# Small inverses applied to the thin factor, one Gram product per chunk, one subtraction per pair: a chunked ridge-attention block with a binarized feed-forward layer

## The chip, the cores and the metric

One core of a Trainium2 chip runs the whole kernel as one program. The metric is device time of one execution in microseconds (us), lower is better. The engines are TensorE (PE: matmuls and transposes, with weight loads listed as PEld), VectorE (DVE), ScalarE (ACT), GpSimd (POOL) and SyncE (SP), which here issues every DMA. Each engine works through its own list in order and waits on semaphores.

## The reference

Four sequences of 1024 rows of 256 numbers go through a layer norm, an attention block and a feed-forward block. Chunks are 128 rows; there are 16 heads of 64.

```python
def step(S, qkv):                      # per head, one chunk after another
    Qc, Kc, Vc = qkv                   # [128, 64] each
    G = Kc.T @ Kc + RIDGE_EPS * I      # 1e-4
    W = jnp.linalg.solve(G, Kc.T @ Vc)
    U = I[:, :8]
    for _ in range(2):
        U, _ = jnp.linalg.qr(W @ U)    # rank 8
    Wr = U @ (U.T @ W)
    S_new = 0.9 * S + Wr
    return (S_new, 0.125 * (Qc @ S_new))
...
x = x + attention(layernorm(x))        # q, k, v = xn @ Wq, Wk, Wv; output @ Wo; its own residual
bw1 = mean(|w1|, per row) * sign(w1)   # w2 alike
x = x + (gelu(layernorm(x) @ bw1.T + b1) @ bw2.T + b2)
```

## The kernel before

The 32 chunks (8 per sequence, which the kernel calls a batch) are worked on singly, in pairs q = 0 to 15, in groups of four g = 0 to 7, and in batches b = 0 to 3. Each engine follows a list that is written out by hand: `PE_ORDER`, `ACT_ORDER`, `DVE_ORDER`, `POOL_ORDER`, `SP_ORDER`. An entry such as `G:14` is one unit of work, and a function of the same table runs it. PE writes a unit into a PSUM place, and ACT or DVE copies it out. The places are three ring banks shared by `XT K V G C X3 H WQ S1 S2`, one double bank `wide` (`ST GI W WT LM`), one `small` (`VS X1 Y YT Z ZT R RP`), one `sum` (`AU`) and one `tok` (`AT`, `O`). A unit waits until the place's unit before it has been copied out.

The way of a chunk:

- `XT` turns the normed rows; `K` and `V` (line 1110, two halves each) make keys and values; `G` (1128) makes the Gram matrices of the 16 heads, `C` the products of keys and values. ACT copies `G` out in two instructions: the leading 32x32 blocks to `lead` (line 690) and the blocks beside them to `rest` (695). SP stores `lead`.
- A pass inverts and factors 128 blocks of 32x32, one on each partition, on DVE: entries `B`, `P:n.0` to `P:n.31` (pivots, lines 916 to 933), `E`, `F`. Passes run in the order (0,0), (0,1), (1,0), (0,2), (1,1), (0,3), (1,2), (1,3), where the first number is 0 for leading blocks and 1 for complements, and the second is the batch. So pass 0 needs `G:0` to `G:7` stored and loaded (`la:0` of SP), pass 1 needs `G:8` to `G:15` (`la:1`), and pass 7 needs `ST:15`.
- For a pair: `VS` and `ST` (1158) make the complement. DVE subtracts it from `rest` (entry `ST`, line 980) in four instructions of 32 partitions each, since for an even chunk and for an odd one the rows lie in other quarters of the partitions. Then `X1`, `GI`, `W`, `WT` (1150) give the solution W, `Y` and `YT` the thin basis, and `Z` = basis-transposed times W the thin right factor (16 heads x 8 rows = 128 rows of 64). DVE masks `Y` and `Z` (984), ACT spreads `YT` and `ZT` (763).
- `LM` (1242, 1246) multiplies the basis into the query weights (the left factor) and into itself: small Gram matrices of the basis, 32 columns wide. `R` (1258) multiplies the right factor into the output weights. Both are stored in DRAM (`sl`, `sr`).
- The small Gram matrices of a batch are loaded (`lm`, four DMAs), inverted on DVE (`M:b.0` to `M:b.7`), stored (`sm`) and loaded as `mb` (`lb`).
- `lp` loads for a pair the right factor, the left factor, the turned rows and the residual. `RP` (1269), one per chunk, multiplies the small inverse into the right factor, 256 columns wide; `AU` (1278) adds the chunk to the running operator; `AT` (1287) applies it.
- `X3`, `H` (1305) and `O` (1317) are the feed-forward part, per group, in half precision with a high and a low part.

In the trace each single-precision matmul is two records, so `R`, 16 matmuls, is 32 records, and `RP`, four matmuls, is 8.

Of the kernel before, what the change touches and what calls it, by code (L numbers as in the profile page):

```python
# [1348 lines left out]
```

## Time and profile before

| | |
|---|---|
| time, three runs | 868.2 us median (865.0 to 872.72) |
| profiled execution | 869.31 us, of which span of the core 867.5 us |
| mean granted TensorE clock | 0.974 |
| PE busy | 771.0 us, 89% |
| DVE busy | 581.7 us, 67% |
| ACT busy | 445.0 us, 51% |
| chain that ended last | PE 31%, DVE 28%, issue 15%, SPq 11%, DMA 10%, ACT 5% |

Busy time counts the union of an engine's instructions; the granted clock is the share of full speed that TensorE got. The chain is followed back from the last instruction, at each step to what released it; "SPq" is time in which SP issued DMAs. Places and times below are counted from the span's start.

### The profile page before, as it was taken

The numbers are of one execution on the slowest core, as the hardware profiler recorded it, in microseconds if no ns is written. First come the engines' busy times: TensorE is split into PE (matmuls) and PEld (weight loads), VectorE is DVE, ScalarE is ACT, GpSimd is POOL, SyncE is SP. The second block draws the span as 40 slices with busy tenths as digits, with TensorE's granted clock in tenths as the row PEclk, the third lists the DMA queues.
The fourth block names the chain that finished last, engine by engine and source line by source line (L and its number), as shares of the span: only waits on it lengthen the run. The fifth ranks groups of instructions, "written<-read, shape, count | busy, mean of one in ns | idle before, by whom it ended". The sixth has DMA issues, their size and how long they took to land.

```text
span 867.5 us, 29412 instructions
## 1 busy us (share of the span) xinstructions
PE 771.0 (89%) x12784; PEld 499.1 (58%) x12784; DVE 581.7 (67%) x1578; ACT 445.0 (51%) x888; POOL 79.6 (9%) x60
## 2 busy tenths in 40 slices
PE   1899999799999989998789889689989999999886
PEld 1355555455455467565566656476667686756563
DVE  3210994289999999999799976679935332565463
ACT  3654554355335345444344436645646647566463
POOL 3100003000300302003003002000020000000000
PEclk9999999899999989999998999999999999999999
DMA  9735313746147645564755656735175632242200
GB/s 265 230 86 76 110 52 114 129 120 137 25 106 125 134 77 109 140 107 125 126 121 120 176 150 197 138 76 121 42 218 108 169 87 81 85 140 74 87 20 30
DMA packets 267315, 100.50 MB, mean 116 GB/s; under 512 B 225457, under 2 KB 260529, under 8 KB 266161
## 3 DMA queue, kind: packets, MB, share of 16 engines
q1 hardware_dynamic: 267184, 98.62, 47.1%
q8 instruction: 100, 1.64, 0.9%
q14 instruction: 31, 0.25, 0.1%
HBM read 53.35 MB, written 45.22 MB: 114 GB/s over the span
## 4 chain that ended last, share of the span: by engine, by line
PE 31%; DVE 28%; issue 15%; SPq 11%; DMA 10%; ACT 5%; POOL 2%; POOLq 0%; DVEq 0%; ACTq 0%
DVE outer L924 11%; DVE ax L933 9%; PE wide L1150 6%; PE tok L1317 5%; PE ring L1305 3%; PE ring L1110 3%; DVE comp L980 2%; PE sum L1278 2%; DVE rd L916 2%; PE tok L1287 2%; SPq L454 2%; PE small L1258 2%; DMA inv_d<-xo 2%; SPq L436 1%; PE ring L1128 1%
## 5 line engine op out<-in xcount | busy, mean ns | idle before, releaser
L1110 PE MATMUL ring<-wkv,xt 128*128 128x512 f32 x512 | 248.5, 625 | 7.4 <-ACT keys L677 3.5
L924 DVE SCALAR_TENSOR_TENSOR outer<-ax,rd 128x448 f32<-128x448 f32 (+15 forms) x368 | 186.1, 533 | 8.8
L933 DVE TENSOR_TENSOR ax<-ax,outer 128x448 f32<-128x448 f32 (+15 forms) x368 | 163.4, 471 | 4.4
L1110 PEld LDWEIGHTS ring<-wkv,xt 128*128 128x128 f32 x512 | 93.7, 195 | 103.8 <-issue 88.4
L1035 DVE TENSOR_TENSOR wkv<-ht,wkv 128x512 f16<-128x512 f32 x64 | 43.6, 689 | 41.7 <-ACT wkv L830 41.3
L579 POOL TENSOR_TENSOR root<-rdc,pos_half 128x32 f32<-128x32 f32 x8 | 43.8, 5474 | 291.4 <-DVE rdc L941 291.4
L683 ACT COPY vals<-ring 128x512 f32<-128x512 f32 x64 | 37.4, 586 | 63.9 <-PE ring L1110 63.5
L1317 PE MATMUL tok<-s2t,wkv 128*128 128x256 f16 x512 | 63.0, 283 | 5.3 <-DVE wkv L1035 3.9
L1305 PE MATMUL ring<-y,s1t 128*128 128x512 f16 x256 | 63.4, 384 | 0.7 <-ACT ht L823 0.6
L823 ACT ACTIVATE ht<-ring,b1c,alpha 128x512 f32<-128x512 f32 x64 | 49.1, 777 | 27.2 <-PE ring L1305 19.6
L1317 PEld LDWEIGHTS tok<-s2t,wkv 128*128 128x128 f16 x512 | 50.8, 101 | 17.3 <-DVE wkv L1035 5.2
L916 DVE RECIPROCAL rd<-ax 128x1 f32<-128x1 f32 x256 | 40.9, 160 | 4.2
L980 DVE TENSOR_TENSOR comp<-rest,wide 32x256 f32<-32x256 f32 x64 | 26.7, 417 | 22.1 <-PE wide L1158 14.0
L865 DVE BATCH_NORM_STATS2 stats<-xg 128x6 f32<-128x256 f32 x32 | 11.2, 414 | 43.1 <-DMA xg<-in_L_attn_x_dram 43.1
L1305 PEld LDWEIGHTS ring<-y,s1t 128*128 128x128 f16 x256 | 23.7, 99 | 28.4 <-issue 3.8
L830 ACT CAST wkv<-ht 128x512 f16<-128x512 f32 x64 | 39.0, 618 | 1.0
L1150 PEld LDWEIGHTS wide<-xf 64*64 64x64 f32 x1024 | 32.1, 138 | 10.5 <-issue 8.2
L1287 PE MATMUL tok<-ac_xn 128*128 128x256 f32 x128 | 34.4, 391 | 4.1 <-ACT ac_xn L799 3.4
L1242 PE MATMUL wide<-wqt,yp 128*32 128x256 f32 x512 | 33.9, 383 | 4.1 <-ACT cut L715 3.6
L1278 PE MATMUL sum<-rp,la 128*128 128x256 f32 x128 | 35.5, 400 | 1.8 <-issue 1.3
L1150 PE MATMUL wide<-xf 64*64 64x64 f32 x1024 | 34.3, 223 | 2.8 <-DMA xf<-inv_d 2.0
L1150 PE MATMUL wide<-giw,resl_c 64*64 64x64 f32 x1024 | 35.0, 225 | 0.5 <-DMA resl_c<-c_d 0.5
(139 smaller groups left out, 1108.4 us busy)
## 6 DMA issues: line engine op xcount, KB each, us to landing
c_d<-cross SPq DMA_DIRECT2D x32, 256.0 KB, 3.2
inv_d<-xo SPq DMA_DIRECT2D x8, 1024.0 KB, 4.7
resl_c<-c_d SPq DMA_DIRECT2D x16, 512.0 KB, 4.9
lm_d<-lm SPq DMA_DIRECT2D x16, 288.0 KB, 3.6
xg<-in_L_attn_x_dram SPq DMA_DIRECT2D x8, 512.0 KB, 4.6
res_d<-xg SPq DMA_DIRECT2D x8, 512.0 KB, 2.7
xt_d<-xt SPq DMA_DIRECT2D x8, 512.0 KB, 3.3
xx<-inv_d SPq DMA_DIRECT2D x64, 64.0 KB, 2.2
```

What stands on the lines that cost most here:

```text
L579: V.tensor_tensor(root[:], rdc[:], pos_half[:], ALU.pow).then_inc(root_ready, 1)
L823: S.activation(ht[:, t % 2], src[:], ACT.Gelu, bias=b1c[:, t:t + 1], scale=alpha1[:, t:t + 1]).then_inc(done, 1)
L916: at = note(V.reciprocal(r, a[:, k, k:k + 1]))
L924: at = note(V.scalar_tensor_tensor(out=t, in0=a[:, k, r0:r1].unsqueeze(2).broadcast_to([P, rows, cols]), scalar=r, in1=a[:, k, r0:HALF + k ...
L933: ends.append(note(V.tensor_tensor(rest, rest, t, ALU.subtract)))
L980: V.tensor_tensor(comp[rows], rest[rows, (2 * q + u) % KEPT], sides[rows], ALU.subtract).then_inc(comp_ready, 1)
L1110: ins = mm(dst[:], xt[:, g % 2, t, P * k:P * (k + 1)], weight[:, t, BANK * j:BANK * (j + 1)], start=t == 0, stop=t == KT - 1)
L1150: ins = mm(dst[half(s), at:at + size], left(s, u, h), right_of(s, u, h), start=True, stop=True)
L1278: ins = mm(dst[:, DM * t:DM * (t + 1)], la[:, n, u, P * t:P * (t + 1)], rp[:, c % 2], start=c % CPB == 0 and t == 0, stop=c % CPB == CPB - ...
L1287: ins = mm(dst[:, 0:DM], xn[:, n, t, P * u:P * (u + 1)], ac[:, c % 2, t], start=t == 0, stop=t == KT - 1)
L1305: ins = mm(dst[:], s1t[:, k, P * t:P * (t + 1)], y3[:, part, k], start=k + part == 0, stop=k + part == KT)
L1317: ins = mm(dst[:, DM * k:DM * (k + 1)], hid[:, part, t, at:at + P], s2t[:, t], start=k + t + part == 0, stop=t + part == FT, skip_group_ch ...
```

## The change

Five things change, and all five orders are written anew.

1. `RP` is gone. `Z` is copied by ACT to `zk` (both halves of the double buffer hold a batch), `ZP` multiplies the small inverse into it (8 matmuls of 32x32 by 64 columns for a pair), DVE masks that, and `ZT` turns it. `R` now makes the finished right factor; ACT scales it into `rp`, and `AU` reads it there. The stores and loads of the right factor through DRAM are gone.
2. `LM`'s small Gram matrices come from one 128x128 by 128 matmul per chunk on a packed copy `ypc` of the turned basis, which ACT makes with a third copy in `YT`. They are stored apart (`m_d`), with a pad row that puts the diagonal blocks at a constant pitch, so one DMA loads them where four did.
3. `G` is copied out to `rest` in four instructions of 32 partitions, so that the rows which the two chunks' complements need lie in one slot.
4. DVE then makes the complement of a pair in one 128-partition subtraction.
5. The orders: both x groups are loaded first, the query weights are turned later, and so on.

```diff
             def gram_out(c):
...
-                    act.wait_ge(comp_ready, 4 * (q + 1))
-                S.copy(rest[:, c % KEPT], blocks[:, :, HALF * (1 - u):HALF * (2 - u)]).then_inc(done, 1)
+                    act.wait_ge(comp_ready, q + 1)
+                across = blocks[:, :, HALF * (1 - u):HALF * (2 - u)]
+                at = 2 * (c // 2) % KEPT
+                for s in range(2):
+                    S.copy(rest[block_rows(s, u), at], across[block_rows(s, u)])
+                    ins = S.copy(rest[block_rows(s, 1 - u), at + 1], across[block_rows(s, 1 - u)])
+                ins.then_inc(done, 1)
...
             def comp_out(q):
-                    for s in range(2):
-                        rows = block_rows(s, 1 - u)
-                        V.tensor_tensor(comp[rows], rest[rows, (2 * q + u) % KEPT], sides[rows], ALU.subtract).then_inc(comp_ready, 1)
+                V.tensor_tensor(comp[:], rest[:, 2 * q % KEPT + 1], sides, ALU.subtract).then_inc(comp_ready, 1)
...
             def left_out(q):       # PE
-                        for f in range(4):
-                            rows, h, at = slice(32 * f, 32 * (f + 1)), 2 * f + odd, BANK * u + DM
-                            ins = mm(dst[rows, at:at + 32], yp[:, u, h], yp[:, u, h], start=False, stop=odd == 1,
-                                     skip_group_check=True, tile_position=(0, 32 * f))
+                for u in range(2):
+                    at = BANK * u + DM
+                    ins = mm(dst[:, at:at + P], ypc[:, u], ypc[:, u], start=True, stop=True, skip_group_check=True)
...
-            def applied(c):
-                dst, done = begin("RP", c)
-                n, u = c // 2 % 2, c % 2
-                pe.wait_ge(apply_loaded[n], 64 * uses_of_slot(c // 2))
-                pe.wait_ge(minv_loaded, 16 * (c // CPB + 1))
-                for f in range(4):
-                    rows = slice(32 * f, 32 * (f + 1))
-                    ins = mm(dst[rows, 0:DM], mb[rows, c % CPB], ra[rows, n, u], start=True, stop=True,
-                             tile_position=(32 * f, 32 * f))
+            def applied(q):
+                dst, done = begin("ZP", q)
+                copied(pe, "Z", q)
+                pe.wait_ge(minv_loaded, 16 * (2 * q // CPB + 1))
+                for u in range(2):
+                    for f in range(4):
+                        rows = slice(32 * f, 32 * (f + 1))
+                        ins = mm(dst[rows, HD * u:HD * (u + 1)], mb[rows, (2 * q + u) % CPB],
+                                 zk[rows, q // PAIRS_B % 2, q % PAIRS_B, u], start=True, stop=True, tile_position=(32 * f, 32 * f))
...
             def right_out(q):      # ACT
                 src, done = begin("R", q)
-                act.wait_ge(r_stored, 16 * q)
-                S.copy(rr[:].rearrange("p u n -> p (u n)"), src[:]).then_inc(done, 1)
+                if q >= 2:
+                    computed(act, "AU", 2 * q - 3)
+                else:
+                    computed(act, "G", NCH - 1)
+                    computed(act, "C", NCH - 1)
+                for u in range(2):
+                    ins = S.activation(rp[:, q % 2, u], src[:, DM * u:DM * (u + 1)], ACT.Copy,
+                                       scale=DECAY ** -((2 * q + u) % CPB))
+                ins.then_inc(done, 1)
...
             def load_apply(q):
-                sp.wait_ge(r_stored, 16 * (q + 1))
-                sp.wait_ge(lm_stored, 16 * (q + 1))
+                sp.wait_ge(left_stored, 16 * (q + 1))
...
-                load(ra[:, n], r_d[both].rearrange("c p n -> p c n")).then_inc(apply_loaded[n], 16)
...
 PE_ORDER = """
-XT:0.0 XT:0.1 WQ:0 WQ:1 K:0.0 K:0.1 K:1.0 K:1.1 K:2.0 K:2.1 G:0 XT:1.0 K:3.0 G:1 XT:1.1 K:3.1 K:4.0 G:2 K:4.1
+XT:0.0 XT:0.1 XT:1.0 XT:1.1 K:0.0 K:0.1 K:1.0 K:1.1 K:2.0 G:0 K:2.1 G:1 K:3.0 K:3.1 K:4.0 K:4.1 K:5.0 K:5.1
```

PE at the very start, before the change (`ident,giw` is a turn of the query weights, `wkv,xt` a key unit, `keys` a Gram unit; x2 of 128x512 is one K unit):

```order
L1103 MATMUL ring<-ident,xh 128x128 x8
L1071 MATMUL ring<-ident,giw 128x128 x8
L1110 MATMUL ring<-wkv,xt 128x512 x12
L1128 MATMUL ring<-keys 64x64 x16
L1103 MATMUL ring<-ident,xh 128x128 x4
```

and with the change:

```order
L1113 MATMUL ring<-ident,xh 128x128 x16
L1120 MATMUL ring<-wkv,xt 128x512 x10
L1138 MATMUL ring<-keys 64x64 x16
L1120 MATMUL ring<-wkv,xt 128x512 x2
L1138 MATMUL ring<-keys 64x64 x16
```

All four turns of rows now come first, and no turn of the query weights stands ahead of the keys.

SP around the load for pass 1 (`ax<-lead_d`), before the change; `resl_c<-c_d` is the load for the first pair's `W`, which waits for the turns of the second feed-forward weight, and `c_d<-cross` here is the store of `C:8`:

```order
L428 DMA inv_d<-xo 128x2048
L401 DMA lead_d<-lead 32x8x32 x2
L436 DMA xx<-inv_d 32x8x64 x8
L401 DMA lead_d<-lead 32x8x32 x4
L478 DMA resl_c<-c_d 128x16x64
L405 DMA c_d<-cross 128x8x64
L418 DMA ax<-lead_d 128x32x32
L436 DMA xx<-inv_d 32x8x64 x4
```

and with the change:

```order
L431 DMA inv_d<-xo 128x2048
L404 DMA lead_d<-lead 32x8x32 x4
L439 DMA xx<-inv_d 32x8x64 x4
L421 DMA ax<-lead_d 128x32x32
L439 DMA xx<-inv_d 32x8x64 x4
L408 DMA c_d<-cross 128x8x64
L481 DMA resl_c<-c_d 128x16x64
```

The load for pass 1 has moved ahead of four side loads, of `C:8`'s store and of the load for `W`.

ACT around the first Gram units, with the change (before, each `lead` row was followed by one row `rest<-ring 128x256`):

```order
L688 COPY lead<-ring 128x256
L696 COPY rest<-ring 32x256
L697 COPY rest<-ring 32x256
L696 COPY rest<-ring 32x256
L697 COPY rest<-ring 32x256
L675 COPY x<-ring 128x512
```

The ring bank of a Gram unit is given back after the fifth instruction instead of the second.

## Rows read from the trace of the kernel before

**Rows 1.** Busy time by stretches; columns: stretch, length, engines' busy us, PEclk, DMA share, GB/s.

```profile
core 0: us, PE busy (x) PEld busy (x) DVE busy (x) ACT busy (x) POOL busy (x), PEclk, DMA share, GB/s
0.00:50.00 50.00, 27.36 (x159) 14.99 (x160) 12.13 (x58) 28.80 (x64) 11.92 (x22) 1.00 0.75 236
50.00:169.00 119.00, 112.32 (x1150) 61.73 (x1148) 56.99 (x167) 57.62 (x113) 11.35 (x6) 1.00 0.42 90
169.00:530.00 361.00, 325.02 (x6558) 208.36 (x6562) 328.35 (x892) 163.86 (x335) 38.97 (x20) 0.96 0.54 120
530.00:650.00 120.00, 104.84 (x2190) 75.67 (x2171) 84.94 (x228) 68.09 (x137) 10.05 (x6) 0.96 0.56 130
650.00:867.50 217.50, 201.46 (x2746) 138.33 (x2743) 99.30 (x235) 126.60 (x242) 7.30 (x7) 0.98 0.32 88
sum 867.50, PE 771.00 PEld 499.07 DVE 581.70 ACT 444.96 POOL 79.58; mean PE 154.20 PEld 99.81 DVE 116.34 ACT 88.99 POOL 15.92
```

**Rows 2.** Timeline, DVE: starts of passes 0 and 1, and `ST:15`.

```profile
86.11 0.20 DVE L911 TENSOR_SCALAR ax<-ax 128x32 f32<-128x32 f32 x1 [23.63 <-DMA ax<-lead_d]
...
169.13 0.20 DVE L911 TENSOR_SCALAR ax<-ax 128x32 f32<-128x32 f32 x1 [8.46 <-DMA ax<-lead_d]
...
530.56 1.76 DVE L980 TENSOR_TENSOR comp<-rest,wide 32x256 f32<-32x256 f32 x4
```

**Rows 3.** Timeline, PE: the waits of the start, in brackets.

```profile
14.79 1.94 PE L1103 MATMUL ring<-ident,xh 128*128 128x128 f32 x8 [14.79 <-DVE xh L903]
19.75 1.97 PE L1071 MATMUL ring<-ident,giw 128*128 128x128 f32 x8 [3.02 <-DMA giw<-in_L_attn_Wq_dram]
21.51 9.02 PE L1110 MATMUL ring<-wkv,xt 128*128 128x512 f32 x16
34.02 3.70 PE L1110 MATMUL ring<-wkv,xt 128*128 128x512 f32 x8 [3.49 <-ACT keys L677]
```

**Rows 4.** Timeline, PE: `G:15`, and the second side unit with what follows.

```profile
149.63 1.15 PE L1128 MATMUL ring<-ra 128*64 128x64 f32 x32
...
170.15 1.08 PE L1158 MATMUL small<-rest,xx 32*32 32x32 f32 x64 [4.67 <-DMA xx<-inv_d]
171.16 3.78 PE L1110 MATMUL ring<-wkv,xt 128*128 128x512 f32 x4
```

**Rows 5.** Timeline, SP: DMA issues between `G:15` and the load for pass 1.

```profile
155.09 1.94 SPq L401 DMA_DIRECT2D lead_d<-lead  x4
157.28 1.06 SPq L478 DMA_DIRECT2D resl_c<-c_d  x1
158.39 1.43 SPq L405 DMA_DIRECT2D c_d<-cross  x1
159.91 1.11 SPq L418 DMA_DIRECT2D ax<-lead_d  x1
```

**Rows 6.** Timeline, PE: back-to-back units; a unit's price is start to next start.

```profile
591.25 1.93 PE L1258 MATMUL small<-wo,zp 128*32 128x256 f32 x32
593.00 0.61 PE L1242 MATMUL wide<-wqt,yp 128*32 128x256 f32 x8
...
594.97 0.63 PE L1203 MATMUL small<-wt,w 128*32 128x64 f32 x32
...
600.11 0.44 PE L1209 MATMUL small<-ident,zm 128*128 128x128 f32 x2
600.38 1.89 PE L1305 MATMUL ring<-y,s1t 128*128 128x512 f16 x8
...
609.43 0.63 PE L1269 MATMUL small<-ra,mb 32*32 32x256 f32 x8
610.00 1.04 PE L1305 MATMUL ring<-y,s1t 128*128 128x512 f16 x4
```

**Rows 7.** Groups by line: busy us, mean ns of one, idle before it.

```profile
L980 DVE TENSOR_TENSOR comp<-rest,wide 32x256 f32<-32x256 f32 x64 | 26.7, 417 | 22.1 <-PE wide L1158 14.0 <-DMA comp_d<-comp 3.0 <-issue 3.0
L727 ACT COPY xf<-small 32x256 f32<-32x256 f32 x64 | 23.2, 363 | 7.7 <-PE small L1158 6.4
L695 ACT COPY rest<-ring 128x256 f32<-128x256 f32 x32 | 12.1, 379 | 0.0
```

More of the change, by code:

```diff
@@ L14 @@
 CPB = SEQ // P
+PAIRS_B = CPB // 2
 NCH = BATCH * CPB
@@ L526, in load_apply @@
                 both = slice(2 * q, 2 * q + 2)
[L527 to L528 removed]
+                load(la[:, n], left_d[both].rearrange("c p n -> p c n")).then_inc(apply_loaded[n], 16)
                 load(xn[:, n], xt_d[g][:, :, 2 * P * n:2 * P * (n + 1)]).then_inc(apply_loaded[n], 16)
@@ L770, in basis, with left_out @@
                     computed(act, "LM", q - 1)
-                spread(yp, src).then_inc(done, 1)
+                spread(yp, src)
+                S.copy(ypc[:].rearrange("p u n -> p (u n)"), src[:, 0:2 * P]).then_inc(done, 1)
             def right(q):
+                src, done = begin("Z", q)
+                if q >= 2 * PAIRS_B:
+                    computed(act, "ZP", q - 2 * PAIRS_B)
+                S.copy(zk[:, q // PAIRS_B % 2, q % PAIRS_B].rearrange("p u n -> p (u n)"), src[:, 0:2 * HD]).then_inc(done, 1)
+            def left_out(q):
+                src, done = begin("LM", q)
+                act.wait_ge(left_stored, 16 * q)
+                act.wait_ge(m_stored, 16 * q)
+                S.copy(lm[:], src[:].rearrange("p (u n) -> p u n", u=2)[:, :, 0:DM + P]).then_inc(done, 1)
+            def applied(q):
                 src, done = begin("ZT", q)
@@ L777, in right @@
                 spread(zp, src).then_inc(done, 1)
-            def left_out(q):
-                src, done = begin("LM", q)
-                act.wait_ge(lm_stored, 16 * q)
-                S.copy(lm[:], src[:].rearrange("p (u n) -> p u n", u=2)[:, :, 0:DM + 32]).then_inc(done, 1)
             def right_out(q):
                 src, done = begin("R", q)
-                act.wait_ge(r_stored, 16 * q)
-                S.copy(rr[:].rearrange("p u n -> p (u n)"), src[:]).then_inc(done, 1)
-            def applied(c):
-                src, done = begin("RP", c)
-                if c >= 2:
-                    computed(act, "AU", c - 2)
-                S.activation(rp[:, c % 2], src[:, 0:DM], ACT.Copy, scale=DECAY ** -(c % CPB)).then_inc(done, 1)
+                if q >= 2:
[7 more added lines that the diff above has]
+                ins.then_inc(done, 1)
             def operator(c):
@@ L991, in basis, with applied @@
                 masked(ym[:], src, done)
-            def right(q):
-                src, done = begin("Z", q)
+            def applied(q):
+                src, done = begin("ZP", q)
                 if q:
@@ L1226, in right @@
                 thin(dst, done, yp, w)
-            def right_turned(q):
-                dst, done = begin("ZT", q)
-                copied(pe, "Z", q)
-                turned_factors(dst, done, zm)
             def left_out(q):
```

283 lines of the change are left out of this document (143 added, 140 removed).

## Prediction

> **What bounds the kernel now.** I read the busy time by stretches first [rows 1]. PE is idle for 867.5 - 771.0 = 96.5 us: 22.6 in the first 50 us, 6.7 up to 169, 36.0 from 169 to 530, 15.2 up to 650 and 16.0 after it. DVE works through 328.35 of the 361 us from 169 to 530, 91%, and through less than half of the last 217. So two engines take turns. Up to 530 the pivot passes on DVE set the pace and PE waits for them; after `ST:15` at 530.56 [rows 2], which lets the last pass begin, PE has a backlog and works at 93%.
>
> Then the timeline of DVE: pass 0 starts at 86.11 after 23.63 us of waiting, pass 1 at 169.13, at the end of a second wait, both for loads of leading blocks [rows 2]. These two dates are not set by DVE. For the first, the timeline of PE [rows 3]: it begins at 14.79, waits 3.02 us for the query weights, starts the keys at 21.51, and waits 3.49 us for ACT, which is held by magnitudes of feed-forward weights that it needs much later. For the second: `G:15` starts on PE at 149.63 and is done at 150.8 [rows 4], but the load that it allows is issued at 159.91 [rows 5]. Between them SP issues the last lead stores up to 157.0, then the load for `W` and the store of `C:8`, which waits for its product. So up to nine of the 18 us from `G:15` to pass 1 are the order on SP.
>
> The sum is made against the profiled execution: 869.31 us, 1.8 over its span and 1.1 over the median of 868.2.
>
> **The change, part by part.** Prices are starts of back-to-back units [rows 6].
>
> *PE work.* One `RP` unit is 610.00 - 609.43 = 0.57 us; 32 go, 18.2 us. `ZP` has no row: 16 matmuls' worth of records, 64 columns, against `Y` with 32 records and 64 columns, 0.63 us at most. Between 0.15 and 0.63 us, I take half, 0.3; 16 units, 4.8 us. `LM`: its group in the page looks costly, but the unit takes 594.97 - 593.00 = 1.97 us and `R`, the same without the small Gram matrices, 593.00 - 591.25 = 1.75: they cost 0.22 us, being packed beside the others. The two full matmuls in their place are four records; a turn of two records of the same size costs 600.38 - 600.11 = 0.27, so 0.54 a unit and +0.32 net, 16 times, 5.1 us more. That part of the change is a loss on PE; between 0 and 10 us, I take 5. PE work falls by 18.2 - 4.8 - 5.1 = 8.3 us.
>
> The Trainium skill, "TensorEngine Tiling (Array Packing)", section Instruction Overhead, says that every matmul carries about 60 cycles of overhead, so that few columns cost no less than 60. By that, an estimate from the page, 16 records of `ZP` would take 0.4 us and the cut of PE work would be 1.6 us smaller; the row of `Y` (32 records in 0.63) is below it.
>
> *DVE work.* The four subtractions of a pair take 1.76 us [rows 2], one of 32x256 417 ns [rows 7]. The length is set by the 256 elements, not by the partitions: on ACT 32x256 takes 363 ns and 128x256 379 [rows 7]. So one is left, 0.42, and 1.34 us go, 16 times 21.4 us, 15 of them inside the DVE-bound stretch. Masks: 16 go, 16 come.
>
> *ACT work.* Four copies of 363 ns for one of 379 [rows 7]: +1.07 us for each `G`, 34 us in all. `ypc`, `zk` and the wider `lm` add about 0.4, 0.4 and 0.2 us a pair, `R` in two pieces replaces two `RP` copies and `rr` is gone: +7 together. ACT rises from 445 to about 486 us. What hides it: in 50 to 169, where `G:4` to `G:15` lie, ACT is busy for 57.6 of 119 us [rows 1]; K, K, G is 1.9 + 1.9 + 1.1 us on PE [rows 3, 4] against about 3.0 on ACT with the new copies. Without that cover it costs 34 us, the second rival.
>
> The Trainium skill, "ScalarE: Activation LUTs", section Rules for kernel authors, budgets about 0.3 us for an activation and 0.83 ns an element. By it, an estimate, a copy of 256 elements would be 0.51 us and the extra 49 us instead of 34; the rows show 0.36 for this copy, and the sum keeps them.
>
> *SP.* 12 issues for small loads, 16 stores and 16 loads of the right factor go, 16 stores come: 28 fewer, at 0.36 to 0.5 us each [rows 5]. I book nothing: after 650 PE has its backlog as cover. The moved load for pass 1 does count, next.
>
> *The start.* x group 1 is loaded before weights, all four turns come first, the query weights leave the head of PE, and the magnitudes come later on ACT. The first product can come about 4 us earlier (DVE's statistics of x group 1 no longer wait behind the weights), the 3.02 us are gone, so the keys start near 16 instead of 21.5; the 3.49 are gone too, and one turn of query weights less (0.9) stands before `C:1`. The four-piece copy of `G:7` gives 1.1 back. Pass 0 starts near 86.1 - 9 = 77 (bounds 74 and 84).
>
> *Pass 1.* From `C:1` to `G:15` PE has the same work in both orders (16 K, 8 G and 6 C each; 13 V against 12). So `G:15` comes near 141, its copies and stores end at 144, four side loads stand ahead of `la:1`, and 169.1 - 159.9 = 9.2 us pass from issue to start: pass 1 starts near 151 to 153, 17 us earlier. Pass 0 (51 us) is over by then, so nothing else is late. Also gone is the wait of 4.67 us at 170.15, after which the next key unit took 3.78 us instead of 1.9 [rows 4]: TensorE was granted its lower clock, 1.2 GHz.
>
> *To ST:15, the meeting point.* On DVE it is 532.3 - 169.1 = 363 us from pass 1 today. Off go 15 x 1.34 = 20, and about 5 for what now stands behind `ST:15` (five short pivots, two additions). 363 - 25 = 338, from 152: 490. On PE it is 532.3 - 21.5 = 511 from the first key; off go 4 us of work (most `RP` lie later), 3.5 and 4.7 of waits and 2 of lower clock, 497 from 16: 513, if its other 30 us of waits stay. They are mostly waits for DVE, which is now 20 us earlier; I let half of them go: 498. I take 498.
>
> *From ST:15 to the end* 335 us remain today. PE still has 13 `R` units where it had 11 and 25 `RP`; `ZP`, `ZT` and `LM` included, 4 us less. The new chain `ZP`, mask, `ZT`, spread, `R`, `AU` is about 4 us longer than `RP`, `AU`, once a batch, but starts from data that is on the chip; FFN units cover it. 331.
>
> Sum: 498 + 331 = 829 us of span, 830.8 of time; against the median 830.
>
> **Rivals.**
>
> *Only PE's own gains count* (chance 0.2). If the 30 us of waits stay, because they come from ACT, DMA and PSUM places and not from DVE, `ST:15` comes at 513: 844 + 1.8 = 846. For it: eight in ten busy tenths on PE even in the DVE stretch. Against it: DVE is busy for 91% there.
>
> *The Gram copies turn ACT and the ring into the bound; slower* (0.07). A Gram unit now holds one of three banks 1.1 us longer. If PE stands still for that time at each of 32 units, 34 us come on PE's path, and the DVE passes start later, not earlier; the start gains 5.5, the rest of DVE's relief is not used: 869 + 34 - 5.5 - 8.3 = 889. It decides from about 1.1 us of stall in 13 of 32 units on, where the 14 us of PE's certain gains are used up. Against it ACT's idle half [rows 1].
>
> *A wash, within 1%* (0.08). The longer ACT and `ZP` chains cost PE waits at pair after pair, 2 us each, 32 us, and eat the 38. Time 862.
>
> *All waits for DVE go* (0.12): `ST:15` at 490 and 10 us of the 31 us of idle after 530 too: 490 + 321 + 2 = 813.
>
> *The forecast* (0.53), own range 820 to 842.
>
> **How the numbers follow.** Range 808 to 856: it holds the forecast, the rival of PE's own gains and the fast case to their edges, and leaves out the two slow ones and a little on the fast side. About 1% is what a measurement of this kernel can tell from no change. Faster by over 1%: 0.53 + 0.2 + 0.12 = 0.85; within 1%: 0.08; slower: 0.07.
>
> **What the next profile would show.** Right: pass 0 starts before 80 and pass 1 before 156; DVE's subtraction is 16 of about 420 ns; `ST:15` lies before 505; PE idle from 150 to 500 is under 30 us; the idle of PE ahead of key units for ACT `rest` stays under 8 us in all. Wrong: key units wait for ACT `rest` again and again (second rival); or DVE waits for PE at `ST` or `Y` entries for tens of us while PE still waits elsewhere (first). What would break the forecast most is the assumption on the 335 us after `ST:15`: if the new orders leave PE without work there at the pairs of batch 3, the gain is given back at the end.

## The result, and the profile after

The changed kernel takes 824.7 us (median of four runs, 823.0 to 831.3), the kernel before 869.6 beside it (865.0 to 872.7): a ratio of 0.950, 95% interval 0.943 to 0.957. The profiled execution has a span of 821.2 us against 867.5. Forecast were 830 us. Medians here are those of the executions in the chip's fast state: one execution each of both_late, old_four_copies and the kernel before lay in a slower one and is left out.

Busy time by the same stretches as in [rows 1]; the columns are stretch, length, busy us of PE, PEld, DVE, ACT and POOL with their instructions, granted clock, DMA share, GB/s:

```profile
0.00:50.00 50.00, 38.08 (x210) 19.96 (x211) 12.12 (x58) 30.18 (x72) 11.93 (x22) 1.00 0.73 227
50.00:169.00 119.00, 106.70 (x1138) 60.89 (x1137) 63.85 (x185) 75.47 (x155) 11.35 (x6) 0.96 0.44 97
169.00:530.00 361.00, 337.57 (x6640) 217.19 (x6638) 321.83 (x890) 202.36 (x423) 42.41 (x21) 0.97 0.58 127
530.00:650.00 120.00, 115.31 (x2497) 88.26 (x2490) 82.81 (x223) 77.87 (x164) 8.88 (x7) 1.00 0.48 115
650.00:821.20 171.20, 158.53 (x1864) 108.42 (x1862) 78.33 (x177) 97.31 (x188) 4.78 (x4) 0.99 0.22 64
sum 821.20, PE 756.20 PEld 494.73 DVE 558.93 ACT 483.20 POOL 79.35; mean PE 151.24 PEld 98.95 DVE 111.79 ACT 96.64 POOL 15.87
```

PE is idle for 65.0 us where it was idle for 96.5: 11.9, 12.3, 23.4, 4.7 and 12.7 us by stretch. Its work is 14.8 us less, ACT's 38 us more, DVE's 23 us less. The same view of after, split at the meeting point that the prediction used, `ST:15`:

```profile
0.00:499.59 499.59, 455.26 (x7693) 281.48 (x7693) 373.04 (x1055) 288.98 (x615) 58.89 (x47) 0.98 0.56 129
499.59:821.20 321.61, 300.93 (x4644) 213.25 (x4644) 185.90 (x476) 194.22 (x386) 20.46 (x13) 0.98 0.36 91
```

and of before:

```profile
0.00:530.56 530.56, 465.26 (x7871) 285.24 (x7872) 398.00 (x1117) 250.34 (x512) 62.79 (x48) 0.97 0.53 124
530.56:867.50 336.94, 305.74 (x4914) 213.83 (x4914) 183.70 (x461) 194.63 (x377) 16.79 (x13) 0.97 0.40 103
```

Up to `ST:15` 31.0 us are gained, 10.0 of work and 21.0 of idle time on PE; behind it 15.3, of which 4.8 are work and 10.5 idle time.

The timeline of DVE, answering to [rows 2]: starts of passes 0 and 1, the complements `ST:0` and `ST:1`, and `ST:15`.

```profile
86.27 0.20 DVE L923 TENSOR_SCALAR ax<-ax 128x32 f32<-128x32 f32 x1 [13.26 <-DMA ax<-lead_d]
...
160.00 0.20 DVE L923 TENSOR_SCALAR ax<-ax 128x32 f32<-128x32 f32 x1 [14.49 <-DMA ax<-lead_d]
...
162.68 0.42 DVE L990 TENSOR_TENSOR comp<-rest,wide 128x256 f32<-128x256 f32 x1 [0.20 <-DVE ax L945]
...
173.08 0.42 DVE L990 TENSOR_TENSOR comp<-rest,wide 128x256 f32<-128x256 f32 x1 [1.68 <-issue]
...
499.59 0.42 DVE L990 TENSOR_TENSOR comp<-rest,wide 128x256 f32<-128x256 f32 x1
```

`ST:15` is 31 us earlier, pass 1 9 us, pass 0 not at all. The gain grows to 25.3 us at the end of pass 4, falls to 17.0 at the end of pass 5 and is 31.0 at `ST:15` (dates of `ST:3` and of the passes' ends, lines 941 and 953, from the same timelines):

| | ST:3 | end of pass 0 | 1 | 2 | 3 | 4 | 5 | ST:15 |
|---|---|---|---|---|---|---|---|---|
| before | 200.1 | 137.2 | 229.0 | 284.5 | 338.8 | 393.2 | 460.7 | 530.6 |
| after | 190.5 | 137.3 | 214.6 | 266.5 | 317.1 | 367.9 | 443.7 | 499.6 |
| four_subs, below | | 138.3 | 221.2 | 276.6 | 328.9 | 381.2 | 456.8 | 518.1 |

From the end of pass 4 to the end of pass 5 DVE waits for 14.6 us with the change and for 4.2 before it; the longest of these waits are for the load of pass 5 (4.9 us), for a `ZP` unit (3.9) and at `ST:11` (3.8). The last step of the row is in part a matter of order: before, `ST:15` stands behind the whole of pass 6, with the change ahead of its last five pivots. The end of pass 6 itself comes 20.7 us earlier (505.6 against 526.3), the start of pass 7 37.7 (510.2 against 547.9).

The start on PE, answering to [rows 3], and the one long wait behind it:

```profile
13.67 1.97 PE L1113 MATMUL ring<-ident,xh 128*128 128x128 f32 x8 [1.54 <-DVE xh L915]
15.44 1.06 PE L1120 MATMUL ring<-wkv,xt 128*128 128x512 f32 x1
...
147.88 3.50 PE L1120 MATMUL ring<-wkv,xt 128*128 128x512 f32 x4 [8.56 <-ACT rest L697]
```

Groups by line, for [rows 7] (busy us, mean ns of one, idle before it):

```profile
L990 DVE TENSOR_TENSOR comp<-rest,wide 128x256 f32<-128x256 f32 x16 | 6.7, 419 | 7.9 <-issue 5.5 <-PE wide L1168 1.8 <-DVE ax L945 0.4
...
L697 ACT COPY rest<-ring 32x256 f32<-32x256 f32 x64 | 23.3, 363 | 0.8
...
L775 ACT COPY ypc<-small 128x256 f32<-128x256 f32 x16 | 6.4, 398 | 0.0
...
L1261 PE MATMUL small<-zk,mb 32*32 32x64 f32 x256 | 6.9, 220 | 1.8 <-DMA mb<-minv_d 1.8
```

The subtraction is 16 instructions of 419 ns. The copies of `rest`, 64 each on lines 696 and 697, take 363 ns of ACT for 32 partitions.

### The profile page after: what moved, and what is told of

Its sections match the earlier page's. It is cut to its first block, busy times and chain, and to the rows that moved or that the text cites. A ratio compares the mean times of both kernels' runs of the same rounds, so it can differ in the third digit from the quotient of the medians.

```text
span 821.2 us, 28518 instructions
## 1 busy us (share of the span) xinstructions
PE 756.2 (92%) x12336; PEld 494.7 (60%) x12336; DVE 558.9 (68%) x1530; ACT 483.2 (59%) x1000; POOL 79.4 (10%) x60
## 4 chain that ended last, share of the span: by engine, by line
PE 49%; DVE 23%; DMA 8%; issue 8%; ACT 5%; SPq 4%; POOL 1%; DVEq 0%; ACTq 0%; POOLq 0%
PE ring L1120 13%; DVE outer L936 8%; PE wide L1160 7%; DVE ax L945 6%; PE tok L1327 6%; PE ring L1138 3%; PE ring L1315 3%; PE wide L1247 3%; PE tok L1297 2%; PE small L1278 2%; PE sum L1288 2%; DMA ax<-lead_d 2%; DMA ax<-comp_d 2%; PE small L1168 2%; DVE rd L928 1%
## 5 line engine op out<-in xcount | busy, mean ns | idle before, releaser
L1120 PE MATMUL ring<-wkv,xt 128*128 128x512 f32 x512 | 245.0, 620 | 9.0 <-ACT rest L697 8.8
L1045 DVE TENSOR_TENSOR wkv<-ht,wkv 128x512 f16<-128x512 f32 x64 | 42.9, 688 | 37.9 <-ACT wkv L842 37.7
L1315 PEld LDWEIGHTS ring<-y,s1t 128*128 128x128 f16 x256 | 23.4, 98 | 27.6 <-ACT ht L835 2.2
L1160 PE MATMUL wide<-resl_c,giw 64*64 64x64 f32 x1024 | 34.5, 224 | 4.7 <-DMA resl_c<-c_d 4.7
L1160 PEld LDWEIGHTS wide<-resl_c,giw 64*64 64x64 f32 x1024 | 32.4, 139 | 7.4 <-issue 5.2
L1160 PEld LDWEIGHTS wide<-giw,resl_c 64*64 64x64 f32 x1024 | 31.1, 135 | 6.2 <-issue 4.2
```

Of the source, the lines that this page charges most:

```text
L1045: V.tensor_tensor(hid[:, 1, t], ht[:, t % 2], hid[:, 0, t], ALU.subtract).then_inc(h_low, 1)
L1120: ins = mm(dst[:], xt[:, g % 2, t, P * k:P * (k + 1)], weight[:, t, BANK * j:BANK * (j + 1)], start=t == 0, stop=t == KT - 1)
L1160: ins = mm(dst[half(s), at:at + size], left(s, u, h), right_of(s, u, h), start=True, stop=True)
L1315: ins = mm(dst[:], s1t[:, k, P * t:P * (t + 1)], y3[:, part, k], start=k + part == 0, stop=k + part == KT)
```

## The experiments

Twelve kernels were run. Medians are beside a kernel before of 869.0 to 870.5 us.

| kernel | built on | median us | ratio to before, 95% interval |
|---|---|---|---|
| al_late | after | 821.8 | 0.941 to 0.948 |
| turn_late | after | 824.1 | 0.943 to 0.951 |
| both_late | after | 824.9 | 0.942 to 0.953 |
| four_subs | after | 842.3 | 0.966 to 0.972 |
| pe_filler | after | 839.0 | 0.963 to 0.969 |
| both_costs | after | 855.2 | 0.980 to 0.989 |
| trip_back | after | 832.9 | 0.951 to 0.962 |
| packed_gram | after | 823.8 | 0.944 to 0.952 |
| packed_al | after | 821.4 | 0.941 to 0.948 |
| old_four_copies | before | 873.7 | 1.000 to 1.008 |
| old_one_sub | before | 865.7 | 0.990 to 0.997 |
| old_load_early | before | 871.4 | 0.999 to 1.003 |

### Do the dates of passes 0 and 1 matter?

The prediction had pass 0 at 77 and pass 1 at 152; they came at 86.3 and 160.0. What held them is plain in the trace. SP of after, in front of the load for pass 0 (line 421):

```profile
65.80 0.51 SPq L378 DMA_DIRECT2D alpha_d<-alpha  x1
74.00 0.34 SPq L380 DMA_DIRECT2D alpha2r<-alpha_d  x1
74.38 0.93 SPq L404 DMA_DIRECT2D lead_d<-lead  x2
75.35 0.45 SPq L408 DMA_DIRECT2D c_d<-cross  x1
79.61 0.60 SPq L421 DMA_DIRECT2D ax<-lead_d  x1
```

Entry `al` stores the scales of the second feed-forward weight and waits until they have landed, 7.7 us, before it issues their load; the last two stores of leading blocks stand behind it. In before it stood ahead of `gs:3` and was over by 61.7. ACT, before pass 1:

```profile
144.28 1.90 ACT L708 COPY xo<-xo 128x1024 f32<-128x1024 f32 x1 [8.26 <-DVE xo L959]
...
147.85 0.37 ACT L688 COPY lead<-ring 128x256 f32<-128x256 f32 x1
...
149.37 0.36 ACT L697 COPY rest<-ring 32x256 f32<-32x256 f32 x1
```

Line 708 is `T:0`, which waits for pass 0 and stands ahead of `G:14` and `G:15` in ACT's order. Both were done on PE by 137.4, but their banks are held until 147.8 and 149.7, and PE's next key unit waits 8.56 us and then takes 3.50 us instead of 1.9, in the lower granted clock.

Three kernels move these entries:

```diff
 SP, al_late
-x:4 al gs:7 cs:1 la:0 cs:2
+x:4 gs:7 cs:1 la:0 al cs:2
 ACT, turn_late                      (both_late: both edits)
-T:0 G:14 G:15
+G:14 G:15 T:0
 SP, turn_late
-gs:13 sa:0 gs:14 gs:15 lx:0 la:1 lx:1
+gs:13 gs:14 gs:15 la:1 sa:0 lx:0 lx:1
```

> The changed kernel; only SP's entry al (store of alpha2, a wait for it to land, load of alpha2r) is moved from ahead of the last lead stores of batch 0 to behind the load for pass 0. Theory 1, the SP order took the 9 us of the start: in the changed kernel al held SP for 8 us, the last lead store was issued at 74.4 though its data lay ready at 69.1; now pass 0 starts near 80 instead of 86.3, pass 1 near 154 instead of 160 since its ACT turn is also earlier, and the time falls by 3 to 7 us against the changed kernel (ratio to before 0.942 to 0.947). Theory 2, pass 0 has slack since PE is the bound from 50 us on: pass 0 starts earlier but the time stays within 1.5 us.

> The changed kernel; ACT's turn of pass 0's result (T:0) stands behind G:14 and G:15 instead of ahead of them, and SP's la:1 ahead of sa:0. Theory 1, T:0 made ACT wait 8.3 us for pass 0 with two full Gram banks behind it, so PE stood 8.6 us and then ran at the lower clock, and pass 1 began 10 us late: now the wait is gone, pass 1 starts near 150, ST:15 near 490, time 5 to 10 us below the changed kernel. Theory 2, the waits only move (side products need the turn anyway): PE idle moves to the first side unit, pass 1 starts earlier, the time changes by less than 2 us.

> Both moves. If the passes set the pace up to ST:15, pass 0 starts near 80 and pass 1 near 148, and the time is 8 to 14 us below the changed kernel (near 812). If PE is the bound, at most the 8.6 us of its standing wait can be won back, and this kernel is no faster than the one with the late turn alone.

Both entries gave their dates back: in both_late pass 0 starts at 79.35 and pass 1 at 148.84. The time did not follow: 821.8 us in al_late, 824.1 in turn_late and 824.9 in both_late, with 824.7 in after. DVE of both_late shows where 11 us went:

```profile
79.35 0.20 DVE L923 TENSOR_SCALAR ax<-ax 128x32 f32<-128x32 f32 x1 [5.63 <-DMA ax<-lead_d]
...
148.84 0.20 DVE L923 TENSOR_SCALAR ax<-ax 128x32 f32<-128x32 f32 x1 [6.05 <-DMA ax<-lead_d]
...
161.67 0.42 DVE L990 TENSOR_TENSOR comp<-rest,wide 128x256 f32<-128x256 f32 x1 [10.34 <-issue]
...
172.07 0.42 DVE L990 TENSOR_TENSOR comp<-rest,wide 128x256 f32<-128x256 f32 x1 [1.67 <-issue]
...
201.69 0.20 DVE L923 TENSOR_SCALAR ax<-ax 128x32 f32<-128x32 f32 x1
```

`ST:0` is subtracted at 161.67 (162.68 in after): DVE's order puts it behind the first pivot of pass 1, so a pass that starts 11 us earlier stands still for 10.34 us at it. Its product comes only 1.0 us earlier, because PE itself waits for the side blocks `xx`, which come from pass 0's result:

```profile
156.24 0.75 PE L1168 MATMUL small<-rest,xx 32*32 32x32 f32 x64 [3.26 <-DMA xx<-inv_d]
...
159.76 1.78 PE L1168 MATMUL wide<-xx 32*32 32x64 f32 x64
```

The row of DVE at 201.69, the start of pass 2, is 1.0 us earlier than in after (202.68). So the wait moved from the load to the first complement, and a start of pass 1 earlier than at 160 brings nothing.

The same move in the kernel before:

```diff
-gs:13 lx:0 lx:1 gs:14 gs:15 l3:0 cs:8 la:1 lx:2
+gs:13 lx:0 gs:14 gs:15 la:1 lx:1 l3:0 cs:8 lx:2
```

> The kernel before; only SP's load for pass 1 stands ahead of the last side load, of the load for W and of the store of C:8. Theory: pass 1 starts near 160 instead of 169, and since DVE sets the pace up to ST:15 the time falls by 5 to 9 us. Rival: PE and the products that the subtractions wait for keep their dates, DVE waits later, under 2 us.

Pass 1 started at 165.5 instead of 169.1 and PE waited 6.8 us for `xx` instead of 4.7; time 871.4, no difference. DVE waited for the product of `ST:1`, in before and then in old_load_early:

```profile
176.47 1.76 DVE L980 TENSOR_TENSOR comp<-rest,wide 32x256 f32<-32x256 f32 x4 [2.73 <-issue]
```

old_load_early:

```profile
179.78 1.76 DVE L980 TENSOR_TENSOR comp<-rest,wide 32x256 f32<-32x256 f32 x4 [9.66 <-PE wide L1158]
```

The old order of DVE has two pivots of pass 1 ahead of `ST:1`, so a pass that starts earlier only waits longer there. The new order has five. With it DVE is busy from 160.0 to 171.4 in after, with these five and `ST:0`, and then waits 1.68 us for `ST:1`. Had pass 1 started at 169.1 as in before, the same work would have ended at 180.5, an estimate, and `ST:1` would come 7.4 us later than at 173.1. So the date of pass 1 has no more than 1.7 us of slack towards later, and nothing is won by an earlier one. No run delayed the pass or changed DVE's order alone.

For al_late alone the four times (821.0 to 822.6) all lie below those of after (823.0 to 831.3), and with packed Gram products the same edit gives 821.4 against 823.8; the intervals overlap, and both_late, which holds the same edit, lies at 824.9. So 2 to 3 us are possible but not shown.

### DVE's subtraction

```diff
-                V.tensor_tensor(comp[:], rest[:, 2 * q % KEPT + 1], sides, ALU.subtract).then_inc(comp_ready, 1)
+                for k in range(4):
+                    rows = slice(HALF * k, HALF * (k + 1))
+                    ins = V.tensor_tensor(comp[rows], rest[rows, 2 * q % KEPT + 1], sides[rows], ALU.subtract)
+                ins.then_inc(comp_ready, 1)
```

> The changed kernel with the subtraction of a pair in four instructions of 32 partitions again (four copies of the Gram matrix stay). It puts 16 x 1.34 = 21 us back on DVE, 20 of them before the last pass begins. DVE theory: ST:15 comes 15 to 20 us later than 499.6, time 12 to 18 us longer (837 to 843). PE theory: DVE has room, under 4 us.

842.3 us, 17.6 more than after, for 16 x 1.3 = 21 us of DVE work. `ST:15` comes 18.5 us later, of which 1.0 is there at the start of pass 0 (DVE of four_subs):

```profile
518.10 1.71 DVE L992 TENSOR_TENSOR comp<-rest,wide 32x256 f32<-32x256 f32 x4
```

So in the new orders most of the DVE work that is added between pass 1 and `ST:15` is time of the kernel. In the old orders the same part was tried by itself, with the copies it needs (old_one_sub), and the copies alone (old_four_copies):

```diff
 both
-                S.copy(rest[:, c % KEPT], blocks[:, :, HALF * (1 - u):HALF * (2 - u)]).then_inc(done, 1)
+                four copies of 32 partitions each
 old_one_sub
-                    for s in range(2):
-                        rows = block_rows(s, 1 - u)
-                        V.tensor_tensor(comp[rows], rest[rows, (2 * q + u) % KEPT], sides[rows], ALU.subtract).then_inc(comp_ready, 1)
+                V.tensor_tensor(comp[:], rest[:, 2 * q % KEPT + 1], sides, ALU.subtract).then_inc(comp_ready, 1)
```

> The kernel before; only the copy of a Gram matrix to rest is split into four of 32 partitions: 32 x 1.1 = 35 us more on ACT, each Gram unit's bank held 1.1 us longer. Forecast's theory, hidden under PE: 0 to 5 us longer. Rival of the slower outcome: 14 to 34 us longer.

> The kernel before with its own orders, and parts 3 and 4 of the change: four copies of 32 partitions into a common slot, one subtraction a pair. DVE loses 21 us, ACT gains 35. If DVE sets the pace to ST:15 and ACT has room, the time falls by 8 to 16 us even in the old orders. If the old orders tie DVE to dates set by PE, by under 4 us, and the gain of the changed kernel needs the new orders.

The copies alone cost 0.4% (873.7 us; 0 to 0.8%), far from the 34 us of the second rival. With the subtraction it is 865.7, 0.3 to 1.0% faster than before: 8 to 9 us better than the copies alone, by the medians about half of the 17.6 that the same subtraction is worth in the new orders. Both are loose: by the ratios and their intervals 5 to 14 us here and 9 to 23 there, so the half isn't shown. The timelines of DVE (`ST:15`) and then of PE of old_one_sub:

```profile
521.16 0.41 DVE L983 TENSOR_TENSOR comp<-rest,wide 128x256 f32<-128x256 f32 x1
```

PE, its waits in brackets:

```profile
33.44 5.40 PE L1113 MATMUL ring<-wkv,xt 128*128 128x512 f32 x8 [3.68 <-ACT keys L677]
...
47.41 5.40 PE L1113 MATMUL ring<-wkv,xt 128*128 128x512 f32 x8 [3.51 <-ACT x L677]
```

The old start is tight on ACT: two key units wait for its copies for 3.68 and 3.51 us and then take 5.40 us; in before the same waits are 3.49 us ([rows 3]) and 1.34, and the units take 3.70. Pass 0 starts at 92.07, 6 us late. `ST:15` still comes 9.4 us earlier than in before. But these waits belong to the copies and don't explain what the subtraction lacks: old_four_copies has them too (3.78 and 3.39 us, pass 0 at 91.66). DVE of old_four_copies:

```profile
539.20 1.76 DVE L984 TENSOR_TENSOR comp<-rest,wide 32x256 f32<-32x256 f32 x4
```

That is 18.0 us behind `ST:15` of old_one_sub, as much as in the new orders. The two profiled executions (877.3 and 860.9 us) lie 3.6 us above and 4.7 below the medians of their kernels, so up to 8 us of the 18 can be chance. Whether the old orders let less of DVE's relief through stays open.

### PE's work

```diff
             def applied(q):                      # pe_filler: ahead of each ZP
                 for u in range(2):
+                    for f in range(4):
+                        rows = slice(32 * f, 32 * (f + 1))
+                        mm(dst[rows, 256 * u:256 * (u + 1)], mb[rows, (2 * q + u) % CPB], zk[rows, ...][:, 0:256], ...)
```

> The changed kernel; ahead of each ZP the products of two old RP units (8 matmuls of 32x32 by 256 columns) are computed and overwritten: 16 x 1.13 = 18 us of PE work back, all but three of the units behind ST:15; nothing else waits for them. If PE is the bound behind ST:15, the time rises by 13 to 18 us. If the end of the kernel is set by chains over DVE, ACT and DMA, by under 5 us.

839.0 us, 14.3 more. The products cost less than was expected (PE of pe_filler, one pair):

```profile
577.86 1.07 PE L1261 MATMUL small<-zk,mb 32*32 32x256 f32 x16
578.74 0.40 PE L1267 MATMUL small<-zk,mb 32*32 32x64 f32 x16
```

They take 0.88 us from start to start, 14.1 us in all and not 18, and PE's busy time rises by 14.5 us, from 756.2 to 770.7. So 14.1 us of added PE work cost 14.3 us of time, one for one. In the profile 5.2 us appear before `ST:15` (504.79), 1.3 of them already at the start of pass 0, the rest behind it. Both costs together:

> The changed kernel with two earlier experiments put together: the complement of a pair in four subtractions again (+21 us of DVE work), and eight products of 256 columns ahead of each ZP (+18 us of PE work; their results are overwritten by the product that follows). Singly they cost 18 and 14 us. Theory: up to ST:15 both engines are near the bound in turns, so the costs mostly add: 32 us less some that hide behind each other, 850 to 856 us. What then remains to the kernel before, 13 to 19 us, is what the written orders give alone. Rival: each relief is only real while the other is there (one meeting point, the later engine decides); then the sum is far less than additive, 842 to 846 us, and the orders give 25 us. The starting phase as the main cause would want at least 17 us to remain, since pass 1 starts 9 us and pass 0 not at all earlier than before.

855.2 us, 30.6 above after; the single costs sum to 31.9. They add, as the theory had it, and the rival of one late engine deciding is out by 9 us at least.

14 to 15 us remain between this kernel and before. That is what is left for the new orders, the dropped traffic, and the costs of the change that stay in. PE is busy for 778.4 us in this kernel against 771.0 in before, ACT for 483.1 against 445.0 and DVE for 581.0 against 581.7: it is faster with more work.

### The traffic of the right factor

```diff
+                load(r_d[both].rearrange("c p n -> p c n"), lm[:, :, 0:DM]).then_inc(r_stored, 16)       # sl
...
+                load(ra[:, n], r_d[both].rearrange("c p n -> p c n")).then_inc(apply_loaded[n], 16)     # lp
```

> The changed kernel with the traffic of the right factor through DRAM put back: per pair one more store of 256 KB behind LM's stores and one more load of 256 KB into an unused buffer, on which AU waits together with the others (the data are those of the left factor). 32 more DMA issues on SP, 8.4 MB. The prediction booked nothing for them, since PE has a backlog after ST:15. By that 823 to 828 us. Rival: PE's idle time after ST:15 fell from 31 to 17 us because SP and the DMA engines are less loaded there; then 14 us come back, 834 to 840 us.

832.9 us, by the medians 8.2 more than after. The two intervals overlap (0.951 to 0.962 and 0.943 to 0.957), but al_late, turn_late, both_late and the two packed kernels, which also do without this traffic, all lie at 821 to 825 us, so a cost is likely; its size is loose. The prediction had booked nothing. The loss isn't all where the rival wanted it. Busy time from the end of pass 5 to `ST:15`, of trip_back and then of after:

```profile
447.43:507.15 59.72, 52.40 (x1364) 37.51 (x1359) 52.14 (x135) 28.79 (x62) 7.54 (x4) 0.94 0.70 188
```

after:

```profile
443.70:499.59 55.89, 50.79 (x1365) 36.87 (x1359) 52.05 (x136) 28.58 (x62) 7.54 (x4) 0.97 0.62 166
```

The same work takes 59.7 us instead of 55.9, with the DMA engines busy for 0.70 instead of 0.62 and the granted clock at 0.94 instead of 0.97: it is the stretch in which the first stores of factors, the loads for `AU` and the last complements meet. Another 3.0 us come behind `ST:15` (324.7 against 321.6), where PE waits 2.2 us for `resl_c<-res_d` and 1.1 for `xf<-inv_d`, 0.5 and nothing in after. The other 3.7 us of the profiled difference are there by the end of pass 5, 2.7 of them by the end of pass 1, ahead of all this traffic: dates vary by that much from run to run (pass 0 starts at 87.9 here, 87.7 in both_costs, 85.8 in packed_gram and 86.3 in after). So I read 5 to 8 us for the traffic.

### The Gram product of the basis

PE of after, one `LM` unit with the units around it, for [rows 6]:

```profile
592.07 1.91 PE L1247 MATMUL wide<-wqt,yp 128*32 128x256 f32 x32
593.91 0.71 PE L1251 MATMUL wide<-ypc 128*128 128x128 f32 x4
594.55 0.43 PE L1261 MATMUL small<-zk,mb 32*32 32x64 f32 x16
594.91 1.26 PE L1327 MATMUL tok<-s2t,wkv 128*128 128x256 f16 x10
```

The unit takes 594.55 - 592.07 = 2.48 us against 1.97 before, `ZP` 0.36. The kernel packed_gram makes the Gram matrices by 32 columns again, but writes each at its diagonal place, so that the single load and everything else stay:

```diff
-                S.copy(ypc[:].rearrange("p u n -> p (u n)"), src[:, 0:2 * P]).then_inc(done, 1)
...
-                for u in range(2):
-                    at = BANK * u + DM
-                    ins = mm(dst[:, at:at + P], ypc[:, u], ypc[:, u], start=True, stop=True, skip_group_check=True)
+                        for f in range(4):
+                            rows, h, at = slice(32 * f, 32 * (f + 1)), 2 * f + odd, BANK * u + DM + 32 * f
+                            ins = mm(dst[rows, at:at + 32], yp[:, u, h], yp[:, u, h], start=False, stop=odd == 1, ...)
```

> The changed kernel with the basis's small Gram matrices made as before, 16 products of 32 columns a pair beside the left factor's, but written at the places of the diagonal blocks, so that the single load stays; the copy ypc on ACT goes. PE work falls by 16 times the difference of the LM units, 2.48 against 1.97 us, 8.2 us, ACT by 6.4 us. By the slope that the filler experiment gave (14 us of time for 18 us of PE work) 6 to 8 us faster than the changed kernel: 817 to 820 us. Rival: the LM units lie where PE waits anyhow or where other work fills in, then no change, 823 to 826 us.

> The kernel packed_gram with SP's entry al moved behind the load for pass 0, as in al_late. If al_late's 3 us are real and independent, 3 us faster than packed_gram: 814 to 817 us. If pass 0's date is worth nothing, the same as packed_gram within 1 us.

PE of packed_gram, the start of one `LM` unit (lines 1246 and 1250) and the `ZP` unit behind it:

```profile
591.60 0.61 PE L1246 MATMUL wide<-wqt,yp 128*32 128x256 f32 x8
...
593.69 0.42 PE L1261 MATMUL small<-zk,mb 32*32 32x64 f32 x16
```

The unit is 593.69 - 591.60 = 2.09 us, so 0.39 less, 6.2 in all; PE's busy time falls from 756.2 to 751.5 us and ACT's from 483.2 to 478.8. The time is 823.8, 0.9 below after: too little to tell from nothing, and below the 4.7 us by which PE's busy time fell, though the work that pe_filler added was paid in full. Why this cut brings nothing isn't shown. packed_al (821.4) is the fastest kernel of the study by its median, 0.3 us before al_late: no difference. Neither is shown to beat the changed kernel; packed_gram shows only that the full product brings nothing that 16 small ones do not.

## Why the prediction was right, and where it wasn't

The date of `ST:15` (498 forecast, 499.6 found) and the time (830, 824.7) came out, but not by all of the steps.

| step | forecast | found |
|---|---|---|
| keys start on PE | 16 | 15.4 |
| pass 0 starts | 77 (74 to 84) | 86.3 |
| pass 1 starts | 151 to 153 | 160.0 |
| worth of pass 1's earlier start | 17 us in the bound on DVE | about 7 us, an estimate |
| DVE's subtraction | 16 x 420 ns, 21.4 us off | 16 x 419 ns; DVE 22.8 us less |
| worth of it | most of 20 us | 17.6 us |
| `ST:15` | 498 | 499.6 |
| `ST:15` to the end | 331 | 321.6 |
| PE's work (busy time) | -8.3 | -14.8 |
| `LM` unit / `ZP` unit | +0.32 / 0.3 us | +0.51 / 0.36 us |
| ACT busy | 486 | 483.2 |
| PE's wait for ACT `rest` | under 8 us | 8.8 us, all but 0.2 in one place |
| traffic of the right factor | 0 | 5 to 8 us, likely |

*The start.* Two steps are wrong. "Pass 0 starts near 86.1 - 9 = 77" moved the products and forgot SP: the keys start 6.1 us earlier as forecast, but `al` had been put between them and the load. "G:15 comes near 141, its copies and stores end at 144" was too late for PE (137.4) and too early for ACT, whose next entry waits for pass 0. In both the order of a third engine was on the path, and the prediction had walked only two of them. al_late and turn_late confirm both causes by their dates.

*And why it didn't matter.* The step "338 us from pass 1 to `ST:15`, from 152: 490" took the stretch as a sum of DVE work from pass 1's start. From 160.0 it was 339.6 us, as forecast. But with pass 1 at 148.8 it is 350.3 us (both_late, `ST:15` at 499.1): an earlier pass waits for PE's products at `ST:0` and `ST:1`. So the 8 us by which pass 1 missed its date cost nothing, and 490 could not be had by that date. At the end of pass 1 the gain is 14.4 us. Of it 3.4 are the earlier product of `ST:1`; 6.3 are the three more pivots that DVE's new order has ahead of `ST:1`, for which the start at 160.0 made room; 4.0 are three cheaper subtractions. Behind `ST:1` DVE waits for 0.2 us in before and for nothing in after. That is read from the traces; no run undid this part of the orders.

*PE's way to `ST:15`*, 498 from the key at 16, is what the forecast took, and here two errors cancel. From the first key to `ST:15` PE took 509.1 us before; 482 were booked and 484.2 found. PE's busy time in it fell by 10.0 us where 6 were booked, its waits by 14.9 (47.5 to 32.6) where 23 were; 8.6 of the waits that are left are the one behind `T:0`. And beside the two waits that the prediction named there were 39 us of others and not 30. That the date came out to 1.6 us is in part luck.

*DVE's relief* was right in mechanism and size: 16 x 1.34 forecast, 17.6 us of time by four_subs.

*Two readings of rows* don't hold, without weight for the sum: PE works at 93% behind 650 [rows 1], but at 91% behind `ST:15` (305.74 of 336.94 us); and the issues in [rows 5] take 0.49 to 1.43 us each, not 0.36 to 0.5.

*Prices.* `ZP` at 0.36 us lies above the 0.3 of the sum and below the 0.4 that the prediction worked out by the Trainium skill. The Trainium skill, "TensorEngine Tiling (Array Packing)", section Instruction Overhead, puts about 60 cycles on every matmul however few its columns; the trace comes near it for `ZP` (16 records of 64 columns in 0.36 us, 22 ns each, 54 cycles at 2.4 GHz), but not for `VS`, whose 64 records of 32 columns take 0.68 us from start to next start at 158.86 in after, 11 ns or 26 cycles each. So the sum is right to go by rows. The copies of `rest` cost 363 ns. The Trainium skill, "ScalarE: Activation LUTs", section Rules for kernel authors, would have given 0.51, an estimate; its budget is for activations, these are plain copies, and the trace decides.

*PE's work.* `RP` went as priced (32 x 0.57). By the unit prices found, the sum is -18.2 + 5.8 + 8.2 = -4.2, yet PE's busy time fell by 14.8 us. The other ten lie in units that the change leaves as they are: their 11504 records sum to 760.7 us by groups before and to 750.0 after. Some 4 to 5 come from the granted clock, 0.978 over 821.2 us against 0.974 over 867.5: that is 36 us at the lower of the two clocks instead of 45. Why the rest of these units is shorter is open. What a microsecond of PE work is worth depends on its place: 14.3 us of time for 14.1 of work in pe_filler, nothing clear for the 4.7 that packed_gram takes away.

*The end.* The 335 us were to shrink by 4 and shrank by 14 to 15. PE waited there for `t` (6.3 us), `resl_c<-res_d` (2.9), `xf` (2.0) and others; after the change 0.5 us for `resl_c<-res_d` are left of these three, and of the 20.7 us of idle time 7.5 are waits for DVE's `wkv`. PE's waits of before behind 530 (total us, times, longest):

```profile
PE small L1158 <- DMA t<-t_d: 6.3, 2, 4.4
...
PE small L1269 <- DMA resl_c<-res_d: 2.9, 1, 2.9
...
PE wide L1150 <- DMA xf<-inv_d: 2.0, 1, 2.0
```

and of after behind 500:

```profile
PE tok L1327 <- DVE wkv L1045: 7.5, 8, 2.8
PE small L1261 <- DMA mb<-minv_d: 1.8, 1, 1.8
```

The term left out was SP's and the DMA engines' load: "I book nothing". trip_back gives about 3 us of it in this stretch; the rest is the new order of the loads or came with the other parts, and no run separates these.

*The rivals.* "Only PE's own gains count" (846) is refuted by four_subs: DVE's relief was used. "The Gram copies turn ACT and the ring into the bound" (889) is refuted by old_four_copies, +3.6 us instead of 34; the one wait for `rest` comes from `T:0` ahead of the copies, and turn_late removes it without any gain. The "wash" and the fast case (813) did not come; the result lies between the forecast and the fast case.

*The whole, added up.* Of 45 us 17.6 are the subtraction in the new orders. `RP`'s 18.2 us of PE work are gone; 14.1 us of such products, put back, cost 14.3, and both costs together 30.6. 5 to 8, if trip_back is read rightly, are the dropped traffic. 6 to 9 are left for the orders, net of what the change costs: the four copies (about 4 us in the old orders) and the 14 us of PE work in the larger `LM` and the new `ZP` units, of which packed_gram takes 6 away and gains 0.9 us, not clear of noise. So the orders' own gain is larger than the 6 to 9 by an unknown part of these, and no run has the new orders without the rest of the change.

## What to carry to other kernels

An earlier start is a gain only up to the first place where the engine that starts meets another one: before booking it, look for the next instruction in its order that waits for somebody else (here `ST:0`, one pivot into pass 1), and walk all engines' orders, SP's blocking waits included, from the last producer to the load. Look also at how much work its order has ahead of that instruction: with two pivots there an earlier pass brought nothing, with five it could use the time. Here an instruction over 32 partitions cost as much as one over 128 (417 against 419 ns on DVE, 363 against 379 on ACT), so merging four into one on the engine that sets the pace paid 17.6 us of 21, though it split one into four on an engine with room. Price a cut by undoing it in the new kernel, and again alone in the old one, with enough executions to tell the two apart: here 17.6 against 8 to 9 us, which four executions against four leave open.

## What the runs showed of the hardware that was not expected

- A copy of 32 partitions x 256 took ACT 363 ns, one of 128 x 256 373 to 398 ns: four times the partitions add 10 to 35 ns. DVE's subtraction: 417 ns for 32 partitions (four_subs) against 419.
- Two full 128-column Gram products, four records, took 0.64 us; sixteen of 32 columns in four tiles cost 0.22 to 0.34 us beside the left factor's products.
- A store of 256 scattered values (`al`) held SP for 7.7 us in after until it had landed, and for 8.3 us in al_late.
- After a wait of 8.56 us TensorE took 3.50 us for a unit that takes 1.9 us: the granted clock is 0.53 from 147.88 to 151.20, TensorE's lower level of 1.2 GHz, and 1.00 behind it. In old_one_sub a wait of 3.68 us was followed by 0.68 over the next 5.4 us, in old_four_copies one of 3.39 us by the same. In before a wait of 3.49 us was followed by 1.00 over the next 3.7 us, so the length of the wait alone didn't decide.
